# Routing of batch 15 ahead of the down products of batch 14, and DMA transposes for half of each routed tile

## What is computed

```python
x = x + xattn(layernorm(x), ctx)       # 8 heads of 64, 512 keys: own tokens and context
h = layernorm(x) * gamma + beta
shared = silu(h @ sw1.T) @ sw2.T       # sw1: 512x256, sw2: 256x512, ternary
probs = softmax(h @ router_w.T)        # 8 experts
top, p = argmax(probs), max(probs)     # each token goes to one expert
routed = p * (silu(h @ ew1[top].T) @ ew2[top].T)
x = x + shared + routed
```

## Time and profile before

| | us |
|---|---|
| median of 3 runs (lowest, highest) | 820.25 (819.57, 821.07) |
| the profiled execution | 821.01 |
| its span, from first to last instruction | 819.3 |
| end of the attention stage, first transpose of a tile, last of them | about 668, 702.6, 797.0 |
| PE, DVE, ACT, POOL busy, share of the span | 83%, 78%, 74%, 70% |

### The profile page before, as it was taken

The page is one execution under the profiler, slowest core; times in us unless marked ns, Lnnn a source line. Parts: engine busy times, 40 slices in busy tenths (PEclk is TensorE's granted clock), DMA queues, the critical chain, the costliest instruction groups (busy, mean ns, idle before and its releaser), DMA issues.

```text
span 819.3 us, 22608 instructions
## 1 busy us (share of the span) xinstructions
PE 681.6 (83%) x7894; PEld 481.3 (59%) x7894; DVE 642.7 (78%) x1411; ACT 604.3 (74%) x1363; POOL 576.9 (70%) x684
## 2 busy tenths in 40 slices
PE   3688779898988999899988898989897765699993
PEld 2355546565656666666656565656565443577772
DVE  3879768888888889788888888888887546688883
ACT  3669567878787978788877878787876631688882
POOL 1356547787878788787878787878786866366664
PEclk9889889999999999999999999999998788899998
DMA  7289858898989999979899899998897842466541
GB/s 257 39 162 174 172 115 158 164 169 168 174 164 166 177 188 163 180 159 185 163 184 160 168 175 174 166 162 165 168 156 155 143 91 93 126 106 106 90 47 15
DMA packets 346307, 121.77 MB, mean 149 GB/s; under 512 B 309898, under 2 KB 341524, under 8 KB 346196
## 3 DMA queue, kind: packets, MB, share of 16 engines
q1 hardware_dynamic: 338388, 110.99, 71.1%
q0 software_dynamic: 7232, 8.79, 6.5%
q10 hardware_dynamic: 576, 0.54, 0.2%
HBM read 30.71 MB, written 14.71 MB: 55 GB/s over the span
## 4 chain that ended last, share of the span: by engine, by line
PE 41%; DVE 21%; issue 13%; DMA 10%; ACT 7%; POOL 7%; SPq 1%; ACTq 1%; DVEq 0%; POOLq 0%
PE FB L358 10%; DMA pt<-p_split 9%; PE TBK L1460 5%; PE S L1388 4%; DVE neg_max L1205 4%; PE S L1563 4%; POOL p_split L571 3%; DVE FB L943 2%; DVE above L948 2%; PE S L1564 2%; ACT k_st L736 2%; ACT p_split L773 2%; DVE v_st L973 2%; DVE hn L1055 2%; POOL g_lo L622 2%
## 5 line engine op out<-in xcount | busy, mean ns | idle before, releaser
L571 POOL TENSOR_TENSOR p_split<-probs,p_split 128x512 f16<-128x512 f32 x256 | 300.2, 1181 | 64.3 <-ACT p_split L773 62.0
L811 ACT ACTIVATE probs<-S,neg_max 128x512 f32<-128x512 f32 x256 | 174.9, 683 | 16.2 <-DVE neg_max L1205 15.0
L773 ACT ACTIVATE p_split<-probs 128x512 f16<-128x512 f32 x256 | 161.0, 629 | 19.2 <-DMA pt<-p_split 17.8
L1205 DVE TENSOR_REDUCE neg_max<-S 128x1 f32<-128x512 f32 x256 | 171.1, 679 | 0.6 <-PE S L1388 0.2
L358 PE MATMUL FB<-xt_hi,w_split 128*128 128x256 f16 x768 | 142.3, 277 | 3.2 <-DVE xt_lo L970 2.9
L1404 PE MATMUL O<-v_st,pt 128*128 128x64 f16 x1024 | 114.6, 195 | 27.2 <-DMA pt<-p_split 26.9
L1404 PEld LDWEIGHTS O<-v_st,pt 128*128 128x128 f16 x1024 | 93.2, 99 | 61.3 <-DMA pt<-p_split 36.7
L1405 PE MATMUL O<-v_st,pt 128*128 128x64 f16 x1024 | 113.9, 195 | 0.0
L1406 PE MATMUL O<-v_st,pt 128*128 128x64 f16 x1024 | 113.9, 194 | 0.0
L1388 PE MATMUL S<-k_st,q_st 64*128 64x512 f16 x768 | 107.1, 385 | 1.1 <-ACT probs L811 1.1
L358 PE MATMUL FB<-xt_lo,w_split 128*128 128x256 f16 x384 | 106.2, 276 | 0.0
(11 more groups left out here) (227 smaller groups left out, 1815.2 us busy)
## 6 DMA issues: line engine op xcount, KB each, us to landing
w_raw<-in_L_ffn_expert_w SPq DMA_DIRECT2D x16, 512.0 KB, 4.5
w_split<-rows SPq DMA_DIRECT2D x39, 132.0 KB, 2.2
c_in<-in_ctx SPq DMA_DIRECT2D x16, 256.0 KB
x_in<-in_x SPq DMA_DIRECT2D x16, 256.0 KB
xb<-in_x SPq DMA_DIRECT2D x16, 256.0 KB, 3.5
pt<-p_split SPq DMA_TRANSPOSE x256, 3.3
out<-rest SPq DMA_DIRECT2D x15, 256.0 KB, 2.5
k_st<-in_L_xattn_Wk SPq DMA_DIRECT2D x2, 512.0 KB, 7.5
```

The source lines that it names most:

```text
L571: g.tensor_tensor(p_split[n % HL_RING][:, 1, :], probs[n % PROBS_RING][:, :], p_split[n % HL_RING][:, 0, :], ALU.subtract).then_inc(p_lo_r ...
L773: a_(p_split[g % HL_RING][:, 0, :], probs[g % PROBS_RING][:, :], ACT.Copy).then_inc(p_hi_ready, 1)
L811: a_(probs[n % PROBS_RING][:, :], S[n % 4][:, :], ACT.Exp, bias=neg_max[:, n % 4:n % 4 + 1], accum_out=sums[:, n % UNITS:n % UNITS + 1]).t ...
L1205: v.tensor_reduce(neg_max[:, n % 4:n % 4 + 1], S[n % 4][:, :], AX.X, ALU.max, negate=True)\
```

## The change

There are two groups of edits. In the end of the attention stage `down_shared(14)` is put behind `route(15)` and `ranks(15)` on TensorE, and on DVE `scale_down(14)` behind `list_tiles`; POOL's addition and store of batch 14's result go behind the scatter of batch 15 (the store was SP's). The scales are computed in a step of their own, `list_scales`, ahead of `through_shared(15, 0)`; `through_shared(15, 1)` now stands behind `list_absent`. ACT writes its zero rows and copies the row scales before the tanh of batch 15. `down_shared(15)` leaves the head of the tile stage and stands in step k = 2, its `scale_down` in step 4. In the tile stage TensorE transposes only the two blocks of the rounded halves, ACT copies only these, and a DMA transpose on SP (`turn_rests`) writes the rests from the row buffer into the other half of `e_ht`; SP's row loads run 3 tiles ahead of its transposes (`LEAD`) in place of up to 16 ahead of the tiles' ends.

```diff
             for a in range(SLOTS):
-                if a >= RING:
-                    sp.wait_ge(e_out, a - RING + 1)
-                load_rows(a)
+                if a + LEAD < SLOTS:
+                    if a + LEAD >= RING:
+                        sp.wait_ge(e_out, a + LEAD - RING + 1)
+                    load_rows(a + LEAD)
+                turn_rests(a)
+            def turn_rests(a):
+                sp.wait_ge(row_in[a % RING], 16 * (a // RING + 1))
+                if a >= HT_RING:
+                    sp.wait_ge(e_up_full, a - HT_RING + 1)
+                sp.dma_start(e_ht[a % HT_RING][:, DC:2 * DC, :], g_rows[a % RING][:, 0:D].bitcast(F16)[:, D:2 * D], transpose=True)\
+                    .then_inc(e_ht_in[a % HT_RING], 16)
...
@@ gpsimd
                     for i in range(TB):
                         scatter_rows(B - 1, i)
-            pool.wait_ge(r_ready, B)
-            g.dma_start(out=out_v[B - 1], in_=rest[(B - 1) % 2][:, :, :]).then_inc(last_r_stored, 16)
-            pool.wait_ge(r_stored, 16 * (B - 1))
-            pool.wait_ge(last_r_stored, 16)
+                    add_x2(B - 2)
+                    store_last(B - 2)
+
+            store_last(B - 1)
+            pool.wait_ge(r_stored, 16 * (B - 2))
+            pool.wait_ge(last_r_stored, 32)
@@ scalar, copy_columns
-                a_(e_ht[a % HT_RING], e_columns.rearrange("p (b t) -> p b t", t=P), ACT.Copy).then_inc(e_ht_ready, 1)
+                a_(e_ht[a % HT_RING][:, 0:DC, :], e_columns.rearrange("p (b t) -> p b t", t=P), ACT.Copy).then_inc(e_ht_ready, 1)
@@ vector, step
+                if k == 4:
+                    scale_down(B - 1)
@@ tensor
                     ranks(B - 1, FB[1])
+                    down_shared(B - 2)
...
-                for c in range(2 * DC):
+                for c in range(DC):
                     last = nc.tensor.transpose(e_columns[:, c * P:(c + 1) * P],
...
             def up(a, s, e):
                 pe.wait_ge(e_ht_ready, a + 1)
+                pe.wait_ge(e_ht_in[a % HT_RING], 16 * (a // HT_RING + 1))
...
                     down(k - 2, r % 2, expert(2))
+                if k == 2:
+                    down_shared(B - 1)
```

More of the change, by code:

```diff
@@ L47 @@
 HT_RING = 4
+LEAD = 3
 ABSENT = 8192
@@ L273, in xattn_ffn @@
         tiles_ready = sem("tiles_ready")
-        absent_ready = sem("absent_ready")
+        scales_listed = sem("scales_listed")
         th_ready = sem("th_ready")
@@ L290, in xattn_ffn @@
         row_in = [sem(f"row_in{i}") for i in range(RING)]
+        e_ht_in = [sem(f"e_ht_in{i}") for i in range(HT_RING)]
         e_turned = sem("e_turned")
@@ L494, in _ @@
                 t = due(n, STORE_R)
-                if t is not None and t < B - 1:
+                if t is not None and t < B - 2:
                     sp.wait_ge(r_ready, t + 1)
@@ L519, in _ @@
             sp.wait_ge(tiles_ready, 1)
+            for a in range(LEAD):
+                load_rows(a)
             for a in range(SLOTS):
-                if a >= RING:
-                    sp.wait_ge(e_out, a - RING + 1)
-                load_rows(a)
+                if a + LEAD < SLOTS:
[3 more added lines that the diff above has]
+                turn_rests(a)
         @block.gpsimd
@@ L613, in scatter_rows, with add_x2, store_last @@
                     .then_inc(scattered[t % 2], 16)
+            def add_x2(t):
+                pool.wait_ge(shared_ready, t + 1)
+                r = rest[t % 2][:, :, :]
+                g.tensor_tensor(r, r, x2[t % 2][:, :, :], ALU.add).then_inc(r_ready, 1)
+            def store_last(t):
+                pool.wait_ge(r_ready, t + 1)
+                g.dma_start(out=out_v[t], in_=rest[t % 2][:, :, :]).then_inc(last_r_stored, 16)
             def gate_scale(t, j):
@@ L626, in _ @@
                 t = due(n, ADD_R)
[L627 to L630, removed]
+                if t is not None and t != B - 2:
+                    add_x2(t)
                 t = due(n, COUNT_AT)
@@ L1158, in list_tiles, with list_scales @@
                 v.memset(pause[:, :], 0.0).then_inc(tiles_ready, 1)
+            def list_scales():
+                EA = [P, SLOTS, E]
+                for c in range(2):
+                    last = v.tensor_tensor(scale_terms[:, c, :, :], owner, spread(up_scale[:, 0:E, 2 + c], EA, 1), ALU.mult)
+                then(last)
+                for c in range(2):
+                    last = v.tensor_reduce(tile_scale[:, :, c], scale_terms[:, c, :, :], AX.X, ALU.add)
+                then(last)
+                v.memset(pause[:, :], 0.0).then_inc(scales_listed, 1)
             def list_absent():
@@ L1170, in list_absent @@
                 also(v.tensor_copy(absent_id, absent))
[L1171 to L1177, removed]
+                dve.wait_ge(dve_step, step[0])
             for n in range(FIRST, LAST):
@@ L1200, in _ @@
                     list_tiles()
+                    scale_down(B - 2)
+                    list_scales()
+                    through_shared(B - 1, 0)
+                    list_absent()
                     through_shared(B - 1, 1)
-                    list_absent()
                 if 0 <= n < NU:
@@ L1263, in _ @@
                 t = due(n, DOWN_AT + 1)
-                if t is not None:
+                if t is not None and t < B - 2:
                     scale_down(t)
@@ L1530, in _ @@
                             .then_inc(rowscale_full, 1)
+                    up_shared(B - 1, 0)
                 t = due(n, DOWN_AT)
-                if t is not None:
+                if t is not None and t < B - 2:
                     down_shared(t)
@@ L1535, in _ @@
                     t = due(n, UP_AT[j])
-                    if t is not None:
+                    if t is not None and (t < B - 1 or j == 1):
                         up_shared(t, j)
```

9 lines of the change are left out of this document (3 added, 6 removed).

## The result

| | before | after |
|---|---|---|
| median of 16 runs each, same chip (us) | 820.44 | 825.18 |
| ratio of the times, 95% interval | 1 | 1.0063 [1.0045, 1.0082] |
| span of the profiled execution (us) | 819.3 | 822.5 |
| first copy of a tile, from the end of batch 14's scatter | 18.20 | 16.70 |
| copy of tile 6, from there | 30.45 | 30.40 |

By the medians the change makes the kernel 4.7 us slower. The end of batch 14's scatter is the last event that the change doesn't touch (684.80 before, 683.47 after; over the profiles of this study it moved between 683.4 and 690.1). From there the two executions differ by 4.55 us: -1.50 at the first copy, +1.45 from it to the copy of tile 6, +4.26 in the 32 steps behind it, +0.34 after the last copy. So I count from this event throughout. Wherever "the trace" is named, starts are read to the nanosecond.

The account below looks back on a forecast made before the run. The prediction took TensorE's sequencer, not its array, to set the tile stage's 2.56 us step. Its terms, -2.7 + 0.7 + 0.5 - 1.1 = -2.6 us, against the median of 820.25 gave 817.6 us, range 813.5 to 822.5.

Parts of the forecast that it names:

- Half of the transposes: Tile stage, TensorE: two transposes less and one wait more save 0.03 us per tile, 1.1 us over 37 tiles.
- if their issue was hidden, the wait costs 1.9: Tile stage: if issuing the transposes cost the sequencer nothing, the added wait loses 1.9 us; no chance given.
- That the sequencer sets the step: Tile stage: the 2.56 us step is the time of TensorE's sequencer and not of its array.
- The head: Start of tile stage: first copy 2.7 us earlier, less 0.7 and 0.5; rival that it gives little, 820.3, chance 0.18.
- the counts' copy: Routing of batch 15: DVE's copy of the counts comes 3.0 us earlier, near 685.6.
- the half clock: First tiles: TensorE, no longer warmed ahead of tile 0, loses 0.5 us over two tiles, ends 0 and 1.5.
- the 4.3 of the other end: Start of tile stage: `list_absent` stays at 4.3 us instead of 2.9, so tile 0's copy gains only 1.1 us.
- The down product of batch 15: Moved among the first tiles, it costs 0.7 us; 1.7 if the array is the bound, 0 if idleness takes it.
- SP: Tile stage: 2.42 us per tile, below 2.56; rival that dearer transpose issues make it the bound, about 831, chance 0.08.
- POOL: Tile stage outputs: a late start is worked off at 1.86 us a tile; rival that it is not, 822.7, chance 0.12.
- The sign named for it: End of tile stage: POOL's last output starting more than 2.5 us behind DVE's last would show the forecast wrong.
- The array: Tile stage rival: TensorE's array is the bound, two transposes fewer give 4.1 us, 815.7 in all; chance 0.17.

Follow-up runs that it names:

- one_wait_more: Kernel before plus one always-met wait ahead of each up product, on row loads already waited for; ratio 1.0047 to the kernel before.
- no_rests: Changed kernel without the DMA transposes and their wait, the products taking the rounded halves twice; ratio 1.0007 to the kernel before.
- head_alone: Kernel before with only the new end of the attention stage and batch 15's down product in step 2, tiles as before; ratio 1.0004.
- banks_b: Kernel before with tiles transposed into two PSUM banks in turn, one wait instruction less per tile; ratio 0.9961 to the kernel before.
- head_all_warm: Kernel before with the new head, three wait instructions taken away (tiles 1 to 8 keep one) and 20 unread products behind tile 0's transpose; ratio 0.9876.
- banks_b_two: Kernel before with two of a step's three wait instructions taken away (two PSUM banks, no output wait of the down product); ratio 0.9936.
- banks_b_all: Kernel before with all three wait instructions of a step taken away, ACT's copy put behind its tanh; ratio 0.9853 to the kernel before.
- rests_all: Changed kernel with a step's wait instructions taken away except that for the rests, two PSUM banks from tile 9 on; ratio 1.0054 to the kernel before.
- after_wait_less: Changed kernel with the up product's two waits on scaled halves replaced by one on tanh, one wait instruction less; ratio 1.0026 to the kernel before.
- rests_lean: Changed kernel with wait instructions taken away except that for the rests, and SP's row-address load without bounds check; ratio 0.9927 to the kernel before.
- head_warm: Kernel before with the new head alone, plus 20 unread products behind tile 0's transpose; ratio 0.9995 to the kernel before.

## Why the prediction was wrong

The forecast was 817.6 and the range ended at 822.5; it became 825.2. Of the sum of -2.6 us:

*Half of the transposes, -1.1, was the step that failed; it is +4.3.* Two sizes were wrong in it. The wait instruction was priced at its record, 0.051; it costs 0.106 (one_wait_more: 0.110 a step). The two transposes were priced at 0.044 for each matmul; they cost the sequencer nothing (no_rests against head_alone). The estimate had spread over all matmuls what the addresses cost. From the first to the eighth they take 0.93 us from start to start, where the prediction had 0.37 for eight records: in the trace the products of the up product, whose weights' address is computed, come in pairs 0.124 apart, of which 0.095 go by between the computation and the first weight load. In banks_b, where no wait stands there, the way from the last address of a down product to the load of the next expert's number is 0.112, with two products and four transposes in it, and that from one address to the next, with two products alone, is 0.112 too: the transposes are free. The text named the other outcome, "if their issue was hidden, the wait costs 1.9", and left it out of the rivals and of the range; with the wait at 0.106 it is 3.9. The rest, some 0.02 to 0.03 a step, lies at the loads of the expert's number. Steps of kernels without DMA transposes differ by as much (2.563 and 2.600); its cause stays open.

*That the sequencer sets the step* was right, and more sharply than the text used it: three wait instructions less took 0.322 off each step.

*The head* is -0.05 at the copy of tile 6 where the sum had -1.5. Its first terms hold: the counts' copy 3.1 earlier (3.0 forecast), the row load 3.3 (3.0), the half clock 0.49 (0.5). The first copy came 1.5 earlier, not 2.7: `list_absent` began 0.3 later than forecast and took 3.85, between the 2.9 taken and the 4.3 of the other end. (The 4.3 had left out the list's last copy, L1170, which ends at 699.69; it is the operation that now took 1.03.) In head_alone that operation took 0.18 and the whole list 3.0, close to the 2.9, and the first copy came 2.1 earlier; at tile 6 nothing was left of that either. The scales beside POOL's addition took 2.43 and not 1.31, but the gate behind them still had to wait for ACT's tanh, so in the changed kernel this cost nothing. Here the port lock that the prediction cited from the Trainium skill (SBUF — State Buffer, § SBUF: two separate sides) agrees with the trace: DVE's short operations end with POOL's long ones (697.76 and 697.72). The full 4.3 that the prediction drew from it did not stay, since with the new order fewer operations of the list stand beside one of POOL. The down product of batch 15 cost 1.6 and not 0.7, the far end of its range.

*SP.* The rival had the right mechanism. Its working for a round, 2.42, is the 2.43 of an undisturbed one; what it lacked was the mean of 2.7, because one issue in five takes 1.3 to 2.2. In the changed kernel SP and the sequencer stand side by side at 2.7, and either alone keeps the kernel slower than before: the wait alone makes it 1.0047, and without the extra wait it is still at 1.0026, with two waits for the rests. *POOL* caught up, as forecast; in head_all_warm, at steps of 2.26, it does not. The sign named for it, a last output over 2.5 us behind DVE's last, could not tell: from start to start it is 3.1 in the kernel before too. *The array* was no bound at steps of 2.56 and more.

## What to carry to other kernels

Where an engine's sequencer sets the pace, count its instructions and not its work: a met wait is dear, a product with a fixed address is nearly free as long as the array has idle time, and a wait whose condition already follows from the order behind another wait should be dropped. Here that gave 1.5%, more than the work moved off the engine ever did. Take start-to-start times from the trace, not durations of records. For a queue that works serially take the mean round under the new load, and ask for each helper how far it is from being the next bound before giving it work.

## What the runs showed of the chip

- A wait instruction of TensorE's sequencer that is met has a record of 51 ns and costs some 0.1 us: the next instruction starts 106 ns behind it (one_wait_more, after), one more made the step 0.110 longer, and three fewer took off 0.094, 0.132 and 0.096 (banks_b, banks_b_two, banks_b_all).
- A DMA transpose of 128x256 f16 between SBUF buffers costs SP 1.19 us at the median and up to 2.2 in the changed kernel (2.8 in rests_lean), a plain load of 132 KB 0.35. The Trainium skill (Advanced Engine Details and Errata, § X-Bar Transpose (TRN2)) calls transposing DMAs as fast as plain ones. Behind the issue the times of after_wait_less are not far from that: 3.1 us (64 KB) and 2.4 us (132 KB) from issue to landing at the median, of which 1.2 and 0.35 are the issue. For the issue itself it does not hold. What lengthens one issue in five stays open.
- The bounds check of a loaded register costs SP 0.3 us per load (undisturbed rounds of 2.43 in rests_all and 2.10 in rests_lean).
- With 4.5 us of unread products in an idle stretch of 5.4 us the granted clock stayed at 1.00 (2.4 GHz, head_warm); in the changed kernel, idle from 696 to 700, it fell to 0.50 (1.2 GHz).
